# Layer 3 of a four-layer graph network: GpSimd joins the statistics of the norm, and batch 15 leaves layer 2 later

## The reference

```python
def _layernorm(x, axis=-1, eps=1e-05):
    m = jnp.mean(x, axis=axis, keepdims=True)
    v = jnp.var(x, axis=axis, keepdims=True)
    return (x - m) / jnp.sqrt(v + eps)
...
        Wh = jnp.einsum('bnf,fo->bno', h, W)
        s1 = Wh @ a1
        s2 = Wh @ a2
        e = s1[:, :, None] + s2[:, None, :]
        e = jnp.where(e >= 0, e, ALPHA * e)
        e = jnp.where(adj_matrix[None] == 0, -jnp.inf, e)
        attention = jax.nn.softmax(e, axis=-1)
        h_prime = jnp.einsum('bij,bjo->bio', attention, Wh)
...
    x = _layernorm(x + _L2_gnn_ref(x, L2_gnn_W, adj), axis=-1)
    x = _layernorm(x + _L3_gnn_ref(x, adj, L3_gnn_W, L3_gnn_a), axis=-1)
```

## Time and profile before

| | us |
|---|---|
| median of three runs | 933.62 (933.27 to 934.35) |
| the profiled execution | 933.39 |
| its span | 931.6 |
| PE busy | 864.7 (93% of the span) |
| DVE busy | 624.1 (67%) |
| ACT busy | 506.6 (54%) |
| POOL busy | 404.0 (43%) |

### The profile page before, as it was taken

One profiled execution on the slowest core, in us unless ns is written; L12 is line 12 of the kernel. 1 busy time (PEld: TensorE's weight loads), 2 busy tenths in 40 slices (PEclk: granted clock), 3 DMA queues, 4 the chain that ended last, 5 costly groups with the idle time before them and its releaser, 6 DMA issues. The chain is left out here.

```text
span 931.6 us, 20358 instructions
## 1 busy us (share of the span) xinstructions
PE 864.7 (93%) x6039; PEld 619.7 (67%) x6039; DVE 624.1 (67%) x1931; ACT 506.6 (54%) x903; POOL 404.0 (43%) x451
## 2 busy tenths in 40 slices
PE   6999999999999999977679999999999998999996
PEld 4799999999999998843344444444444444777775
DVE  4756645545545556467676887778876652899997
ACT  4332221211211236566457787888877667888884
POOL 4010211211111225300435788887887776456554
PEclk9999999999999999999979999999999999999999
DMA  9100000000010000000133443333433430010111
GB/s 253 35 9 15 13 12 12 24 12 13 23 30 4 13 1 0 0 0 1 34 70 69 87 102 86 68 78 81 99 82 69 87 86 1 13 34 23 34 34 45
DMA packets 34249, 40.82 MB, mean 44 GB/s; under 512 B 6673, under 2 KB 17553, under 8 KB 34193
## 3 DMA queue, kind: packets, MB, share of 16 engines
q1 hardware_dynamic: 32816, 39.87, 17.9%
q10 hardware_dynamic: 1376, 0.27, 0.1%
HBM read 6.43 MB, written 4.19 MB: 11 GB/s over the span
## 5 line engine op out<-in xcount | busy, mean ns | idle before, releaser
L1686 POOL TENSOR_TENSOR half_sum<-prob 128x1024 f32<-128x1024 f32 x64 | 151.4, 2378 | 21.3 <-PE bank L1950 18.4
L1761 ACT ACTIVATE prob<-wide 128x1024 f32<-128x1024 f32 x128 | 124.1, 1022 | 38.4 <-PE wide L1942 38.1
L460 ACT CAST yT<-wide 128x512 fp32r<-128x512 f32 x48 | 28.1, 589 | 190.8 <-PE wide L870 141.9
L1830 DVE CUSTOM_DVE_ANT_0 junk<-wide,mask_ij 128x512 bf16<-128x512 f32 x128 | 82.8, 684 | 51.2 <-PE bank L1922 50.7
L1938 PE MATMUL wide<-qk_st 128*128 128x512 f32 x256 | 84.5, 437 | 4.9 <-ACT prob L1761 3.3
L1830 DVE CUSTOM_DVE_ANT_0 junk<-bank,mask_ij 128x512 bf16<-128x512 f32 x128 | 83.0, 686 | 0.0
L553 POOL TENSOR_TENSOR Xr<-Xf,Xr 128x512 fp32r<-128x512 f32 x16 | 20.4, 1293 | 140.1 <-ACT Xr L455 139.9
L1496 PEld LDWEIGHTS bank<-Wh,pr 128*128 128x128 f32 x512 | 65.2, 191 | 14.0 <-ACT pr L1349 6.5
L1496 PE MATMUL bank<-Wh,pr 128*128 128x129 f32 x512 | 68.5, 278 | 4.8 <-ACT pr L1349 4.2
L59 PE MATMUL bank<-z,L3T_hi 128*128 128x256 f32 x256 | 72.4, 283 | 0.4 <-DVE z L678 0.4
L61 PE MATMUL bank<-z,L3T_lo 128*128 128x256 f32 x256 | 72.3, 283 | 0.0
(11 more groups left out here) (302 smaller groups left out, 2392.0 us busy)
## 6 DMA issues: line engine op xcount, KB each, us to landing
qk_st<-qkT SPq DMA_DIRECT2D x192, 128.0 KB, 2.4
out_dram<-rc SPq DMA_DIRECT2D x15, 256.0 KB, 2.3
Xf<-X SPq DMA_DIRECT2D x14, 256.0 KB, 2.3
A<-in_adj_dram SPq DMA_DIRECT2D x4, 256.0 KB, 5.0
qk_st<-neg_row SPq DMA_DIRECT2D x64, 2.0 KB
Xf<-in_x_dram SPq DMA_DIRECT2D x2, 256.0 KB, 7.0
mask_q<-mask_ji SPq DMA_DIRECT2D x16, 32.0 KB, 1.8
w<-in_L_gnn_W_dram SPq DMA_DIRECT2D x2, 128.0 KB, 2.2
```

The source lines that it names most:

```text
L460: act.copy(yT[bb][i][0][:], psum_y[i][:]).then_inc(y_hi, 1)
L1686: pool.tensor_tensor(flat(half_sum[h][:]), flat(prob[bp][h][:, 0:2]), flat(prob[bp][h][:, 2:4]), ALU.add).then_inc(h_sum, 1)
L1761: act.activation(flat(prob[bp][h][:, 2 * half:2 * half + 2]), wide[half][:], ACT.Exp, scale=SCALE).then_inc(t_exp, 1)
L1830: dve.tensor_tensor_reduce(out=junk[h % 2][:], in0=ROWS[h][:], in1=m.mask_ij[:, i], scale=1.0, scalar=3.0 * MASKED, op0=ALU.add, op1=ALU.m ...
```

## The change

The four `bn_aggr` per batch (item B) leave VectorE's list in layer 3, but for batch 15. In their place GpSimd, in the new `pool_root`, joins the two halves of each row with seven small operations on 128x4 numbers and one that adds the two variance terms, before the power that it made already. The mean is half the sum of the half means, the variance is (sum of both sums)/128 + (difference of the means)^2/4.

At the meeting of the layers the texts of `tail` change, and one more step of layer 3 is written out on VectorE and ScalarE ahead of b.15 and y.15. In the loops nothing else moves. The line of `pairs` changes the rounding of the first step, for the new starting steps.

```diff
-    lead = max(lead, first - first % 2)
+    lead = max(lead, first + first % 2)
...
-    DVE_ORDER = staged("m0:0 m1:0 d0:2 e0:1 e1:1 r0:2 m2:0 e2:1 e3:1 m3:0 r1:2 d1:2 c0:0 c1:0 r2:2 r3:2 b:2 B:2")
+    DVE_ORDER = staged("m0:0 m1:0 d0:2 e0:1 e1:1 r0:2 m2:0 e2:1 e3:1 m3:0 r1:2 d1:2 c0:0 c1:0 r2:2 r3:2 b:2")
...
+    def pool_root(pool, b, par):
+        stats, aggr, rstd, w = norm.stats[par], norm.aggr[par], norm.rstd[par], terms[par]
+        means, sums = (stats[:, :, 1], stats[:, :, 4]), (stats[:, :, 2], stats[:, :, 5])
+        pool.wait_ge(norm.s_stats, after(b, 4))
+        pool.wait_ge(norm.s_x, after(b - 2, 4))
+        hold(pool, gate)
+        pool.tensor_tensor(w[:, 0], means[0], means[1], ALU.subtract).then_inc(s_joined, 1)
+        pool.tensor_tensor(w[:, 1], means[0], means[1], ALU.add).then_inc(s_joined, 1)
+        pool.tensor_tensor(w[:, 2], sums[0], sums[1], ALU.add).then_inc(s_joined, 1)
+        pool.wait_ge(s_joined, after(b, JOINED, 1))
+        pool.tensor_tensor(w[:, 3], w[:, 0], w[:, 0], ALU.mult).then_inc(s_joined, 1)
+        pool.wait_ge(s_joined, after(b, JOINED, 3))
+        hold(pool, gate)
+        pool.tensor_scalar(aggr[:, :, 0], w[:, 1], 0.5, 1.0, ALU.mult, ALU.mult).then_inc(s_joined, 1)
+        pool.tensor_scalar(w[:, 2], w[:, 2], 1.0 / D, EPS, ALU.mult, ALU.add).then_inc(s_joined, 1)
+        pool.wait_ge(s_joined, after(b, JOINED, 4))
+        hold(pool, gate)
+        pool.tensor_scalar(w[:, 3], w[:, 3], 0.25, 1.0, ALU.mult, ALU.mult).then_inc(s_joined, 1)
+        pool.wait_ge(s_joined, after(b, JOINED, 7))
+        pool.tensor_tensor(rstd[:], w[:, 2], w[:, 3], ALU.add).then_inc(norm.s_eps, 1)
+        pool.wait_ge(norm.s_eps, after(b, 1))
+        pool.tensor_tensor(rstd[:], rstd[:], m.neg_half[:, 0:NT], ALU.pow).then_inc(norm.s_rstd, 1)
...
-        norm.root(pool, b + CREDIT, par)
+        pool_root(pool, b, par)
...
# ScalarE
-                 "E2.15 E3.15 f.14 3W1.0 e.14 y.13 E4.15 E5.15 E6.15 E7.15 3G.0 3L0.0 3L1.0 3XR.1 3L2.0 3L3.0 3X.1 f.15 e.15 "
-                 "3E0.0 3W0.1 3W1.1 y.14 3E1.0 3XR.2 3G.1 3L0.1 3L1.1 3X.2 3L2.1 y.15", ACT_ORDER, work, item)
-            pairs(act, B, 4, third.in_order(item, third.act_order), last=B, first=3)
+                 "E2.15 E3.15 f.14 3W1.0 e.14 E4.15 E5.15 y.13 E6.15 E7.15 3G.0 3L0.0 3L1.0 3XR.1 3L2.0 3L3.0 3X.1 f.15 e.15 "
+                 "3E0.0 3W0.1 3W1.1 3E1.0 3XR.2 y.14 3G.1 3L0.1 3L1.1 3X.2 3L2.1", ACT_ORDER, work, item)
+            third.in_order(item, third.act_order)(3, 1, [True] * 4, 1)
+            tail("y.15", ACT_ORDER, work, item)
+            pairs(act, B, 4, third.in_order(item, third.act_order), last=B, first=4)
...
# VectorE
-                 "3m0.1 3m1.1 3e2.0 3e3.0 c1.15 c2.15 3m2.1 3m3.1 3c0.1 3c1.1 b.15", DVE_ORDER, work, item)
-            pairs(dve, B, 3, third.in_order(item, third.dve_order), last=B, first=2)
+                 "3m0.1 3m1.1 3e2.0 3e3.0 c1.15 3m2.1 3m3.1 3c0.1 3c1.1 c2.15", DVE_ORDER, work, item)
+            third.in_order(item, third.dve_order)(2, 0, [True] * 3, 1)
+            tail("b.15", DVE_ORDER, work, item)
+            pairs(dve, B, 3, third.in_order(item, third.dve_order), last=B, first=3)
...
# TensorE
-                 "t2.15 3i.0 t3.15 d.14 o.14 3x.1 V0.15 V1.15 V2.15 V3.15 3j.1 D0.15 D1.15 3q0.0 3q1.0 d.15 3w0.1 3q2.0 "
+                 "t2.15 3i.0 d.14 o.14 t3.15 3x.1 V0.15 V1.15 V2.15 V3.15 3j.1 D0.15 D1.15 3q0.0 3q1.0 d.15 3w0.1 3q2.0 "
```

More of the change, by code:

```diff
@@ L1179, in layer3 @@
     rec = [over(f"rec3{k}", [P, NT]) for k in range(2)]
+    terms = [over(f"terms3{k}", [P, 4, NT]) for k in range(2)]
     at[0] = 205120
@@ L1199, in layer3 @@
     stored = [sem(f"stored{k}") for k in range(2)]
+    s_joined = sem("halves_joined")
     last_eps, last_rstd, last_x, last_stored = (sem(f"last_{x}") for x in ("eps", "rstd", "applied", "stored"))
@@ L1202, in layer3 @@
     LAST = B - 1
+    JOINED = 7
     out_bank = [bank[6], bank[7]]
@@ L1264, in pool_constants @@
         norm.credit_apply(pool)
+        pool.sem_inc(s_joined, CREDIT * JOINED)
         pool.wait_ge(*ready["O"])
@@ L1281, in pool_last_root @@
             two = slice(2 * h, 2 * h + 2)
-            pool.wait_ge(norm.s_aggr, after(LAST, 4, 2 * h + 2))
+            pool.wait_ge(norm.s_aggr, CREDIT * 4 + 2 * h + 2)
             hold(pool, gate)
@@ L1414, in item @@
                 norm.statistics(dve, b + CREDIT, par, r[par])
-            elif what == "B":
-                norm.aggregate(dve, b + CREDIT, par)
         return item
```

## The result

| | before | after |
|---|---|---|
| median | 933.62 | 944.1 (runs 941.94 to 944.19) |
| the profiled execution | 933.39 | 944.19 |
| its span | 931.6 | 942.3 |
| PE busy | 864.7 | 864.1 (92%) |
| DVE busy | 624.1 | 619.9 (66%) |

The ratio is 1.0098 [1.0082, 1.0114]: slower by 1%. A fifth run at 2898.84 us was disturbed; the ratio leaves it out, the median does not. VectorE has less work and the kernel is slower, as forecast (941.2), but terms of the sum were wrong in opposite directions.

What follows compares the result with a forecast made beforehand. VectorE's list set layer 3's pace; after the change GpSimd's ring would. First norm, longer root, half clock before x.4, five rounds at 0.81 and the end, less what is absorbed, made 933.4 + 7.8 = 941.2 us; range 933 to 944.5.

Steps and rivals of the forecast that it cites:

- The ring through GpSimd's copy: Layer 3 loop: copy, x, statistics, norm, copy over two steps; 16.35 us before, 18.0 after, above 17.19, setting the pace.
- So the root takes 2.45 + 1.03 = 3.5 us: GpSimd's layer 3 root: eight spacings (0.81, 0.84, 0.8) plus the power; norm 1.65 later, round +0.81.
- low bound: Shortest GpSimd root: 0.13 for free spacings, 0.28 for the other five, 2.83 us in all, norm later by 1.0.
- signs of being wrong: Copies 17.2 apart or closer, first norm before 803, or GpSimd's small operations following each other in 0.2 or less.
- rival A: Layer 3: VectorE sets the pace, GpSimd's idle time hides the root; step toward 8.3, 927 to 930.5; chance 0.16.
- Without the wait that is full speed. By my count all that follows comes 1.65 earlier: Layer meeting: with y.13 out of E4.15's way, t3.15 loses its 1.61 wait and takes 1.20, not 1.93.
- E1.0 then waits for e3 and a0.0 gains 0.4 more: Layer meeting: y.14 leaves E1.0's way; a0.0, which waited 1.34, comes another 0.4 earlier.
- The 2.85 are lost again at this place, +0.1: First norm of layer 3: statistics gain 2.85, but g2.15 waits for late b.15; norm at 804.7 against 804.57.
- Half clock before x.4: TensorE idles some 4 us before x.4, then runs at half clock: 1.4 lost, bounds 0 and 1.4.
- B: Rival, a draw: spacings near the low bound, ring loses 0.1 a round, meeting keeps a microsecond; 932 to 935.5; chance 0.11.
- C: Rival, plain delay: the ring as forecast, but the clock doesn't fall before x.4; 939.8; chance 0.15.
- D: Rival: the layer meeting gives nothing, first norm up to 2.8 later than forecast; 943 to 944; chance 0.08.

Runs made afterwards that it cites:

- e4: Kernel after, with GpSimd's copy of a batch one norm earlier: 937.54 us, ratio 1.0043.
- e8: Kernel before, with the change's root on GpSimd and the copy one norm earlier, old orders kept: 934.12 us, ratio 1.0008.
- e7: Kernel before, with only GpSimd's copy one norm earlier: 934.21 us, ratio 1.0010.
- e3: Kernel after, with c2.15 back behind c1.15 on VectorE and y.14 back ahead of E1.0 on ScalarE: 940.28 us, ratio 1.0074.
- e1: Kernel before, with the change's GpSimd root alone and the old orders where the layers meet: 936.27 us, ratio 1.0037.
- e5: Kernel before, joining dropped from VectorE, a three-operation GpSimd root using only half of each row (no candidate): 931.89 us, ratio 0.9981.
- e2: Kernel after, with the old root and the joining back on VectorE, so the new orders alone: 939.69 us, ratio 1.0075.
- e11: Kernel after, with only c2.15 back in its old place on VectorE: 944.0 us, ratio 1.0111.
- e12: Kernel after, with only y.14 back ahead of E1.0 on ScalarE: 941.95 us, ratio 1.0101.
- e6: Kernel before, with the change's root lengthened by four more small waiting operations, old orders kept: 949.9 us, ratio 1.0173.

## Why the prediction came out, point by point

- **The ring through GpSimd's copy sets the pace: right.** From x.6 on every x waits for its copy (rows above), and e4 and e8 remove the loss by moving the copy alone. VectorE set the pace before: right (e7).
- **"So the root takes 2.45 + 1.03 = 3.5 us": mis-sized.** It is 2.86, near my low bound of 2.83. For the three free spacings I had taken the 0.27 of a pair of tensor_scalar, 0.81 in all; two of them are tensor_tensor and took 0.155, and all three took 0.59. The three with one wait took 0.71, not 0.84, as the first of them took only 0.16. The two with a wait and a hold took 0.53, not 0.8: that is the largest of the three errors. The norm comes 1.0 later, not 1.65. The round is +0.4, not +0.81. By my sum, 2.86 makes a ring of 17.36, and measured are 17.56 to 17.59, so 0.2 of it I had too short. One of my signs of being wrong did come: small operations that follow each other in 0.2 or less. It was not enough for rival A, which needed a root of 2.69.
- **"Without the wait that is full speed. By my count all that follows comes 1.65 earlier": mechanism right, size wrong.** The wait went; its worth is 0.46, since the clock behind it is full in five of six kernels with that order. The 0.73 of half clock were that one execution's, and the 2.85 at the statistics of batch 0 was too high by that as well.
- **"E1.0 then waits for e3 and a0.0 gains 0.4 more": the step that failed.** I had seen that c2.15 must wait for y.14 and counted it as nothing, without asking who waits for c2.15. a0.0 does: it lost 2.45 in waiting (3.79 against 1.34) and half clock behind it. From x.0 to x.4 that chain is worth 3.3 (56.8 against 53.4 in e3), and 2.8 to the end.
- **"The 2.85 are lost again at this place, +0.1": right against the trace of before, and too small against full clock.** In e3, where the chain is mended, the first norm starts +0.07 later than in that trace, but 1.9 later than in e1. In the kernel after it starts 3.4 later than before from x.0, by the failed step.
- **Half clock before x.4: right** (0.58 behind 3.69 of idle time).
- **The sum from x.0.** To x.4: forecast +2.3, measured +4.9. To the statistics of batch 2: forecast +2.6, measured +5.4 (61.98 to 67.39). The five rounds from there to the statistics of batch 12: forecast +4.1, measured +2.05. The rest: forecast +1.1, measured +0.9. Forecast 7.8, measured 8.3: an oversized root and a missed wait nearly cancelled, and the slow clock in the trace of before hid another 1.1. The total was good partly by luck.
- **Rival A falls** twice: the root hid only where the copy was moved, and with the ring out of the way a step takes 8.5, not 8.3. e5 took 0.54 a step off VectorE with hardly anything put in its place, and got 0.2% of the kernel. The Trainium skill ("Perfetto Trace Analysis", Identifying the Most-Contended Engine) advises to optimize the engine with the highest occupancy first, and for TensorE it doesn't count matmul busy time as such. By e5 that advice was worth little here.
- **Rivals B, C and D.** B falls, the round lost 0.4. C falls, since the clock did drop behind the wait at x.4. D had the first norm up to 2.8 later and 943 to 944: that is nearest to what was measured (3.4 later, 944.1), though D said only that the meeting gives nothing, not which wait takes it.
- **Open:** the 2.35 us ahead of x.0; why one execution drops the clock behind 1.61 of idle time and five others don't; what b.15 in its old place alone would give; and what holds the step at 8.5.

## What to carry to other kernels

Before work moves to an engine with idle time, ask what stands behind it on that engine's list and who waits for that: here a copy, and moving the copy made the same work free inside the loop. Where items of one stage are put later, follow each of them to its readers and to every wait in the code that stands on it; an item that "only waits a little" held up the whole matmul engine, and by a wait that asked for more than the item behind it needed. And a clock level read behind one wait in one execution is not a price: it should be seen twice before it goes into a sum.

## What the hardware showed that I had not expected

- On GpSimd tensor_tensor on 128x4 that don't wait for the one just ahead start 0.155 apart, and two tensor_scalar 0.28 apart. A tensor_tensor that waits for the one just ahead starts 0.28 behind it as well. All are shown as 0.20 long, so form and waits decide, not the busy time.
- Behind the same 1.61 us of idle time TensorE ran t3.15 in 1.93 us in one kernel's trace and in 1.16 in another's. Behind 3.7 to 3.8 us its clock fell to half in all six kernels that have such a wait (after, e2, e3, e4, e11, e12), and behind some 2.0 in five of six steps of e6.
- Waits of TensorE amplify each other: 1.1 us more of a small operation's chain cost 2.4 us in three of four rounds (17.56 to 20.02), since the longer wait brought the lower clock, and 1.2 in the round where the clock stayed full (18.73).
